# A Perceiver block with 16 experts: layer-norm rows ahead of their low parts, the last expert rows sent by the load queue, shared down products in four banks

## The chip, the cores and the metric

The kernel runs on one core of one Trainium2 chip, in one launch. The metric is the time of the whole program on the device in microseconds (us), the median of several runs. On the core five engines run at once, each with its own instruction stream, and wait for each other only on semaphores: TensorE (PE, matrix products; its weight loads are listed apart as PEld), VectorE (DVE), ScalarE (ACT), GpSimd (POOL) and SyncE (SP, which here does nothing but issue DMAs). A DMA is issued by the sequencer of an engine into that engine's own queue ("SPq", "ACTq") and carried out by 16 DMA engines that all queues share. PSUM, where PE writes its products, has 8 banks of 512 floats for each of 128 partitions.

## The reference

Three residual steps on `x` (8 batches of 64 tokens, width 512): a cross attention over 512 context rows, a linear attention, and a mixture of experts. The change lies in the third and in the layer norm before it.

```python
x = x + xattn(layernorm(x), ctx, ctx)
x = x + linear_attention(layernorm(x))       # ends in  out @ w_out + b_out
x = x + ffn(layernorm(x))

def ffn(h):                                  # E = 16 experts, cap = 8 tokens of each batch for each expert
    scores = softmax(h @ gate_w.T).transpose(0, 2, 1)
    topk_w, topk_idx = top_k(scores, cap)
    x_tok = take_along_axis(h, topk_idx)     # 64 slots (8 batches x 8) for each expert
    g, u = x_tok @ Wg[e].T, x_tok @ Wu[e].T  # 512 -> 1024
    eo = (gelu(g) * u) @ Wd[e].T * topk_w    # 1024 -> 512
    out = scatter_add(eo at topk_idx)
    shared = (gelu(h @ Ws_g.T) * (h @ Ws_u.T)) @ Ws_d.T
    return out + shared
```

## The kernel before, in words

All engines' programs are written out by hand, in order. The 512 tokens stand as NT = 4 tiles of 128.

**From the second attention to the router.** PE multiplies `att_T` by `w_out` tile by tile (`residual`, L1217) into banks 4 to 7. For each tile DVE (`residual_ln`) adds the bank to `x` (L723), takes the statistics (`ln_stats`, L703 to L705), has ACT take a square root (`ln_std`, L457), and finishes the normalised rows `xn_moe` (`ln_rows`, L711 to L715). PE transposes a tile's rows into bank t (`moe_transpose`, L1321). Products that need more precision than one pass gives are made of two parts: ACT copies the transposed tile rounded into `xn_hi` (`xn_high_tile`, L462), and DVE subtracts that from the bank into `xn_lo_moe` (`xn_low_tile`, L735). In DVE's program the low part of tile t-1 stands between the statistics and the rows of tile t (argument `behind`). Then PE makes 48 small products of the router (L1399, 32 columns each; those of tile t wait for its low part), DVE picks the tokens, and PE gathers them into `x_slot`.

**The items.** What follows is a list of 24 items: one eighth of the shared network ("shared item", s0 to s7) and the 16 experts (e0 to e15), in the order s0, e0, e1, s1, e2, e3, s2, ..., e12, e13, s7, e14, e15. Item n writes its gate product into bank 2*(n%2) and its up product into the bank after it; ACT takes the gelu (L638), DVE multiplies (L949). For an expert PE transposes the result (L1365, bank 4 + n%2), ACT copies it into `hid_T` (L654) and PE multiplies by `w_d` (L1376, bank 6 + n%2). For a shared item PE makes 4 down products of 3 passes each, one for each token tile (L1389), and DVE adds each to `x` (`item_sum`, L965, semaphore `sx_done`). They go into banks 4 + n%2 and 6 + n%2 in turn, so the third waits for the sum of the first and the fourth for the sum of the second. PE's order in a step is gate of n, transposes of n-1, up product of n, down product of n-1.

**The loads.** SP issues three loads of 2 MB for each expert (`expert_load`, L394), each as soon as PE has used the buffer of the expert two before. The very last is `w_d` of e15, after the down product of e13.

**The rows.** An expert's output (64 slots by 512) must be regrouped by batch: 8 small DMAs, one for each batch b, of 8 rows of 2 KB each into `eo_slot[:, b]`. The place of `eo_slot[:, b]` holds the low parts of the shared weights of s_b until that item is done, so a batch's rows can be sent only from then on. ACT issues them (`send`, L649) between its other work. In its program, after the cast of s7's hidden part and before the copy into `hid_T` of e14, stand 21 of them: b = 7 of e0 to e12, and all 8 of e13. The 8 of e14 come after it, then gelu of e15. When all have landed PE multiplies by `give` (L1469), which puts the rows of 15 experts back to their tokens; then come the transposes, the down product and the `give_last` product (L1476) of e15, DVE's last sums and the output.

```python
            def shared_down_bank(n, t):
                return (4, 6)[t % 2] + n % 2
```

Of the kernel before, what the change touches and what calls it, by code (L numbers as in the profile page):

```python
# [25 lines left out]
NT = TOK // P  # L26
# [12 lines left out]
def perceiver_block(nc, x_d, ctx_d, wq_d, bq_d, wk_d, bk_d, wv_d, bv_d, wo_d, bo_d, wqkv_d, proj_d,  # L39
                    wout_d, bout_d, gate_d, wg_d, wu_d, wd_d, wsg_d, wsu_d, wsd_d, out_d):  # L40
    main = ExitStack()
    with main:
# [292 lines left out]
        def experts_upto(n):  # L335
            return n + 1 - shared_before(n + 1)
# [3 lines left out]
            return experts_upto(n) + NT * shared_before(n + 1)  # L340

        def shared_down_bank(n, t):
            return (4, 6)[t % 2] + n % 2

        def qkv_bank(n):
            return n % 4 if n < 8 else n - 4
# [7 lines left out]
        @block.sync  # L354
        def _(sp):
            for dt in range(KT):
                sp.dma_start(wk_raw[:, dt], wk_d[:, dt]).then_inc(wk_in[dt], 16)
                sp.dma_start(ctx_raw[:, dt], ctx_d[0, :, dt]).then_inc(ctx0_in[dt], 16)
            for tile, src in ((bias_k, bk_d), (bias_q, bq_d), (bias_v, bv_d)):
                sp.dma_start(tile[:], src).then_inc(bias_in, 16)  # L360
            sp.dma_start(wv_raw[:], wv_d).then_inc(wv_in, 16)
            sp.dma_start(x[:], x_d.rearrange("(t p) d -> p t d", p=P)).then_inc(x_in, 16)
            sp.dma_start(wq_raw[:], wq_d).then_inc(wq_in, 16)
            sp.dma_start(bo_rows[:], bo_d.partition_broadcast(P)).then_inc(rows_in, 16)
            with sp.Fori(1, B) as b:
                sp.wait_ge(ctx_split, b + KT - 1)
                sp.dma_start(ctx_raw[:], ctx_d[b]).then_inc(ctx_in, 16)
            sp.dma_start(w_o[:], wo_d).then_inc(wo_in, 16)
            sp.dma_start(w_qkv[:], wqkv_d).then_inc(wqkv_in, 16)
            sp.wait_ge(x_done, NT)  # L370
            sp.dma_start(bout_rows[:], bout_d.partition_broadcast(P)).then_inc(rows_in, 16)
            for q in range(4):
                sp.dma_start(proj_twice[HD * q:HD * (q + 1)], proj_d[q % 2]).then_inc(proj_in, 16)
            sp.dma_start(w_out[:], wout_d).then_inc(wout_in, 16)
            sp.wait_ge(xbias_done, 2 * NT)
            sp.dma_start(gate[:], gate_d).then_inc(gate_in, 16)
            sp.wait_ge(qkv_lo_dve, KT)
            sp.wait_ge(qkv_lo_pool, 2 * KT)
            sp.dma_start(ws_g[:], wsg_d).then_inc(wsg_in, 16)
            sp.wait_ge(kv_ps, NT * KT)  # L380
            sp.dma_start(ws_u[:], wsu_d).then_inc(wsu_in, 16)
            sp.dma_start(w_u0[:], wu_d[0]).then_inc(wu_in[0], 16)
            sp.dma_start(w_d0[:], wd_d[0]).then_inc(wd_in[0], 16)
            sp.dma_start(ws_d[:], wsd_d).then_inc(wsd_in, 16)
            sp.wait_ge(att_done, 2 * NT)
            sp.dma_start(w_g0[:], wg_d[0]).then_inc(wg_in[0], 16)
            def expert_load(kind, e):

                tiles, src, arrived, used = {"g": (w_g, wg_d, wg_in, g_ps), "u": (w_u, wu_d, wu_in, u_ps),
                                             "d": (w_d, wd_d, wd_in, down_ps)}[kind]  # L390
                if e >= 2:
                    n = AT["e", e - 2]
                    sp.wait_ge(used, downs_upto(n) if kind == "d" else n + 1)
                sp.dma_start(tiles[e % 2][:], src[e]).then_inc(arrived[e % 2], 16)  # L394

            expert_load("g", 1)
            expert_load("u", 1)
            for e in range(2, E, 2):
                for kind, ahead in (("g", 0), ("u", 0), ("g", 1)):
                    expert_load(kind, e + ahead)  # L400
                if e == 2:
                    sp.wait_ge(give_ps, 2)
                    sp.wait_ge(last_T_done, NT)
                    expert_load("d", 1)
                for kind, ahead in (("d", 0), ("u", 1), ("d", 1)):
                    expert_load(kind, e + ahead)
            for t in range(NT):
                sp.wait_ge(y_done, t + 1)
                sp.dma_start(out_d[P * t:P * (t + 1), :], x[:, t, :]).then_inc(out_sent, 16)
            sp.wait_ge(out_sent, 16 * NT)  # L410
# [42 lines left out]
        def _(act):  # L453
# [171 lines left out]
            act.wait_ge(wsd_in, 16)  # L625
            shared_high_gu(0)
            shared_high_d(0)
            for t in range(NT):
                ln_std(2, (t,))
                if t:  # L630
                    xn_high_tile(t - 1)
            xn_high_tile(NT - 1)
            act.wait_ge(lsub_done, 1)
            act.activation(logit[:], logit[:], ACT.Exp).then_inc(lexp_done, 1)

# [3 lines left out]

            def send(n):  # L640

                ready, free = experts_upto(n - 1), shared_before(n + 1)
                was_ready, was_free = experts_upto(n - 2), shared_before(n)
                for e in range(ready):
                    if e >= was_ready:
                        act.wait_ge(eo_done, e + 1)
                    for b in range(0 if e >= was_ready else was_free, free):
                        row = SLOTS * (e % 2) + CAP * b
                        act.dma_start(eo_slot[CAP * e:CAP * (e + 1), b, :], eo_of(e)[row:row + CAP, :]).then_inc(eo_sent[e % 2], 16)  # L649

            def item_out(n):
                if is_expert(n):
# [31 lines left out]
                if split_next:  # L684
                    shared_high_d(earlier[1] + 1)
            item_out(LAST - 1)
            send(LAST)
            item_gelu(LAST)
            item_out(LAST)

# [2 lines left out]
        def _(dve):  # L693
# [21 lines left out]
                dve.tensor_scalar(xn[:, t, :], x[:, t, :], mean_var[:, t, 0:1], r,  # L715
                                  ALU.subtract, ALU.mult).then_inc(xn_done, 1)

            def residual_ln(k, xn, behind=None):

                for t in range(NT):  # L720
                    dve.wait_ge(xbias_done, NT * (k - 1) + t + 1)
                    dve.wait_ge(res_ps, NT * (k - 1) + t + 1)
                    dve.tensor_tensor(x[:, t, :], bank(RES_BANK[k - 1] + t), x[:, t, :], ALU.add).then_inc(x_done, 1)  # L723
                    dve.wait_ge(x_done, NT * (k - 1) + t + 1)
                    ln_stats(t)
                    if behind and t:
                        behind(t - 1)
                    ln_rows(k, t, xn)
                if behind:
                    behind(NT - 1)  # L730

            def xn_low_tile(t):
                toks = slice(P * t, P * (t + 1))
# [202 lines left out]
            dve.tensor_tensor(gate_lo[:], gate[:], gate_hi[:].bitcast(F32), ALU.subtract).then_inc(gate_split, 1)  # L936
            shared_low_gu(0)
            shared_low_d(0)
            residual_ln(2, xn_moe, xn_low_tile)


            def over_experts(v):
# [114 lines left out]
        def _(pe):  # L1057
# [156 lines left out]
            def residual(k, rows_T, w, behind=None):  # L1214
                for t in range(NT):
# [1 line left out]
                        ins = pe.matmul(bank(RES_BANK[k] + t), rows_T[:, dt, P * t:P * (t + 1)], w[:, dt, :],  # L1217
                                        start=(dt == 0), stop=(dt == KT - 1))
                    ins.then_inc(res_ps, 1)
                    if behind and t:  # L1220
                        behind(t - 1)

            pe.wait_ge(o_done, B)
            pe.wait_ge(wo_in, 16)
# [96 lines left out]
                    ins = pe.transpose(ps[:, t, P * dt:P * (dt + 1)], xn_moe[:, t, P * dt:P * (dt + 1)], ident[:])  # L1321
                ins.then_inc(xnT_ps, 1)

            residual(1, att_T, w_out)
            for t in range(NT):
                moe_transpose(t)

            def item_up(n, weights, shared_parts, off, in_, done, steps=range(KT)):


                dst = 2 * (n % 2) + off
                if is_expert(n):
                    e = ITEMS[n][1]
                    pe.wait_ge(in_[e % 2], 16 * (e // 2 + 1))
# [33 lines left out]
            def item_down(n):  # L1368
# [11 lines left out]
                else:  # L1380
                    i = ITEMS[n][1]
                    pe.wait_ge(ws_split, 3 * i + 3)
                    pe.wait_ge(hid_split, shared_before(n) + 1)
                    for t in range(NT):
                        if t >= 2:
                            pe.wait_ge(sx_done, NT * shared_before(n) + t - 1)
                        rows = slice(P * t, P * (t + 1))
                        for j, (a, c) in enumerate(((hid_hi, ws_d_hi[:]), (hid_lo, ws_d_hi[:]), (hid_hi, ws_d_lo[:, i, :]))):
                            ins = pe.matmul(bank(shared_down_bank(n, t)), a[:, n % 2, rows], c, start=(j == 0), stop=(j == 2))  # L1389
# [136 lines left out]
```

## Time and profile before

| | |
|---|---|
| median of 3 runs | 713.93 us (712.55 to 715.34) |
| the profiled execution's own time | 714.17 us |
| its span, first to last instruction | 712.4 us |
| PE busy | 661.5 us, 93% of the span |
| DVE busy, ACT busy | 318.2 us, 250.8 us |
| mean granted TensorE clock | 0.971 |

The span is what the trace covers; the 1.8 us more are start and end outside of it. Busy shares are means over stages with different limits, so the stages around the change are read one by one. "Granted clock" is 1.00 at TensorE's full 2.4 GHz and 0.50 at 1.2 GHz.

### The profile page before, as it was taken

Reading aid. Unit: us, or ns where it says so; the run is one execution under the profiler, and the core shown is the slowest. Engines: PE = TensorE matmul, PEld = TensorE weight load, DVE = VectorE, ACT = ScalarE, POOL = GpSimd, SP = SyncE. Lnnn points to the kernel's source line nnn. Section 1 sums busy time; section 2 is a strip of 40 time slices with the busy share of each in tenths; the row PEclk is TensorE's granted clock in tenths of the full one; section 3 lists DMA queues with packets and bytes.
Section 4 is the critical chain, followed back from the end, with each engine's and each line's share of the span. In section 5 each row is a group of like instructions: output and inputs, shape, how many; then the busy total and the mean of one; then the engine's idle time right before and its main releaser. Section 6 shows DMA issues by size and latency. Waiting matters only on the chain.

```text
span 712.4 us, 10361 instructions
## 1 busy us (share of the span) xinstructions
PE 661.5 (93%) x4224; PEld 427.2 (60%) x4224; DVE 318.2 (45%) x646; ACT 250.8 (35%) x479; POOL 31.8 (4%) x33
## 2 busy tenths in 40 slices
PE   6999999999999999799989499989999999999966
PEld 5767778777787875578875285353544434354422
DVE  5965554636445165657786532423233231323302
ACT  4644545536454351547752113111220221122000
POOL 0300000000000000750000000000000000000000
PEclk9999999999999999899999769999999999999989
DMA  8111101010700000311196200889999999999921
GB/s 300 69 60 60 49 13 60 1 61 1 296 0 2 1 2 1 104 47 76 28 428 276 97 0 15 339 352 422 424 405 403 409 404 396 398 386 390 367 73 61
DMA packets 14347, 129.55 MB, mean 182 GB/s; under 512 B 2720, under 2 KB 2848, under 8 KB 6240
## 3 DMA queue, kind: packets, MB, share of 16 engines
q1 hardware_dynamic: 12384, 126.95, 45.3%
q10 hardware_dynamic: 1920, 1.97, 0.9%
q8 instruction: 33, 0.54, 0.3%
q14 instruction: 10, 0.08, 0.0%
HBM read 125.90 MB, written 1.05 MB: 178 GB/s over the span
## 4 chain that ended last, share of the span: by engine, by line
PE 78%; DVE 10%; ACT 4%; DMA 2%; ACTq 2%; issue 2%; SPq 1%; DVEq 0%
PE ps L1072 21%; PE ps L1337 14%; PE ps L1376 8%; PE ps L1347 5%; PE ps L1253 4%; PE ps L1142 4%; PE ps L1389 3%; PE ps L1217 2%; PE ps L1118 2%; ACTq L649 2%; PE ps L1153 2%; PE ps L1183 2%; PE ps L1290 2%; PE ps L1399 1%; PE ps L1302 1%
## 5 line engine op out<-in xcount | busy, mean ns | idle before, releaser
L1376 PE MATMUL ps<-w_d,hid_T 128*64 128x512 f32 x256 | 59.6, 609 | 9.6 <-ACT hid_T L654 8.2
L1337 PE MATMUL ps<-w_g,x_slot 128*64 128x512 f32 x256 | 58.1, 595 | 0.7 <-ACT x_slot L673 0.7
L1337 PE MATMUL ps<-w_u,x_slot 128*64 128x512 f32 x256 | 58.0, 595 | 0.0
L503 ACT ACTIVATE probs<-ps,neg_max 128x512 f32<-128x512 f32 x64 | 43.5, 686 | 39.1 <-DVE neg_max L788 39.1
L638 ACT ACTIVATE hid<-ps 128x512 f32<-128x512 f32 x24 | 14.3, 598 | 113.9 <-PE ps L1337 79.6
L768 DVE COPY probs_T<-ps 128x512 f32<-128x512 f32 x32 | 22.1, 692 | 68.7 <-PE ps L1142 68.7
L1072 PE MATMUL ps<-wv_hi,ctx_hi 128*128 128x512 f32 x128 | 51.6, 403 | 0.2 <-ACT v_s L484 0.2
L1072 PE MATMUL ps<-wv_lo,ctx_hi 128*128 128x512 f32 x128 | 50.0, 391 | 0.0
L1072 PE MATMUL ps<-wv_hi,ctx_lo 128*128 128x512 f32 x128 | 49.9, 390 | 0.0
L788 DVE TENSOR_REDUCE neg_max<-ps 128x1 f32<-128x512 f32 x64 | 39.7, 683 | 18.4 <-PE ps L1118 18.3
L949 DVE TENSOR_TENSOR hid<-hid,ps 128x512 f32<-128x512 f32 x24 | 16.5, 686 | 70.2 <-PE ps L1337 34.3
L1376 PEld LDWEIGHTS ps<-w_d,hid_T 128*64 128x64 f32 x256 | 18.1, 140 | 45.2 <-issue 35.9
L1072 PE MATMUL ps<-ctx_hi,wk_hi 128*128 128x512 f32 x112 | 44.4, 397 | 0.4 <-ACT k_T L488 0.4
L1072 PE MATMUL ps<-ctx_lo,wk_hi 128*128 128x512 f32 x112 | 43.6, 390 | 0.0
L1072 PE MATMUL ps<-ctx_hi,wk_lo 128*128 128x512 f32 x112 | 43.6, 389 | 0.0
L1337 PEld LDWEIGHTS ps<-w_g,x_slot 128*64 128x64 f32 x256 | 17.9, 137 | 35.4 <-issue 34.3
L488 ACT ACTIVATE k_T<-ps,bias_k 128x512 f32<-128x512 f32 x32 | 21.6, 689 | 48.8 <-PE ps L1072 48.8
L1337 PEld LDWEIGHTS ps<-w_u,x_slot 128*64 128x64 f32 x256 | 18.0, 137 | 33.5 <-issue 33.5
L667 ACT COPY x_slot<-ps 64x512 f32<-64x512 f32 x14 | 8.1, 580 | 80.8 <-PE ps L1376 80.8
L1072 PEld LDWEIGHTS ps<-wv_hi,ctx_hi 128*128 128x128 f32 x128 | 24.0, 188 | 16.6 <-ACT v_s L484 6.3
L781 DVE TENSOR_SCALAR probs<-probs,row_inv 128x512 f32<-128x512 f32 x64 | 31.1, 487 | 2.3
L1142 PE MATMUL ps<-ident,probs 128*128 128x128 f32 x256 | 31.0, 274 | 0.0
(218 smaller groups left out, 1215.2 us busy)
## 6 DMA issues: line engine op xcount, KB each, us to landing
w_u<-in_wu SPq DMA_DIRECT2D x16, 2048.0 KB, 15.3
w_d<-in_wd SPq DMA_DIRECT2D x16, 2048.0 KB, 11.3
w_g<-in_wg SPq DMA_DIRECT2D x16, 2048.0 KB, 12.5
ctx_raw<-in_ctx SPq DMA_DIRECT2D x7, 1024.0 KB, 4.8
w_qkv<-in_wqkv SPq DMA_DIRECT2D x1, 3072.0 KB, 15.2
ws_g<-in_wsg SPq DMA_DIRECT2D x1, 2048.0 KB, 7.8
ws_u<-in_wsu SPq DMA_DIRECT2D x1, 2048.0 KB, 7.8
ws_d<-in_wsd SPq DMA_DIRECT2D x1, 2048.0 KB, 21.9
```

Source lines behind the costliest of these rows:

```text
L488: act.activation(k_T[:, ht, :], bank(FIRST_K + ht if first else PROJ[ht % 2]), ACT.Identity, bias=bias_k[:, ht:ht + 1], scale=1.0).then_in ...
L503: act.activation(probs[:, p, :], bank(SCORE[p]), ACT.Exp, bias=neg_max[:, p:p + 1], scale=1.0, accum_out=row_sum[:, p:p + 1]).then_inc(exp ...
L768: dve.tensor_copy(probs_T[:, ht % 2, 1].rearrange("p s c -> p (s c)"), bank(TRANS[ht % 2][1])).then_inc(pT_done[1], 1)
L781: dve.tensor_scalar(probs[:, p, :], probs[:, p, :], row_inv[:, p:p + 1], None, ALU.mult).then_inc(prob_done, 1)
L788: dve.tensor_reduce(neg_max[:, p:p + 1], bank(SCORE[p]), AX.X, ALU.max, negate=True).then_inc(max_done, 1)
L1072: ins = pe.matmul(dst, a(dt), c(dt), start=(dt == 0 and i == 0), stop=(dt == KT - 1 and i == 2))
L1142: ins = pe.transpose(ps[:, TRANS[ht % 2][pr], P * st:P * (st + 1)], probs[:, 2 * ht + pr, P * st:P * (st + 1)], ident[:])
L1253: ins = pe.matmul(bank(qkv_bank(n)), a, c, start=(dt == 0 and i == 0), stop=(dt == KT - 1 and i == 2))
L1337: ins = pe.matmul(ps[64 * fh:64 * (fh + 1), dst, :], x_slot[:, e, dt, :], weights[e % 2][:, dt, BANK * fh:BANK * (fh + 1)], start=(dt == 0 ...
L1347: ins = pe.matmul(bank(dst), a, c[:, dt, :], start=(dt == 0 and j == 0), stop=(dt == KT - 1 and j == 2))
L1376: ins = pe.matmul(ps[64 * fh:64 * (fh + 1), 6 + n % 2, :], hid_T[:, n % 2, j, 64 * fh:64 * (fh + 1)], w_d[e % 2][:, KT * fh + j, :], start ...
L1389: ins = pe.matmul(bank(shared_down_bank(n, t)), a[:, n % 2, rows], c, start=(j == 0), stop=(j == 2))
```

## The change

Three places, independent of each other. (1) DVE makes the rows of all four tiles before any low part, ACT's square roots and high copies are interleaved to match, and PE transposes tile 0 between the third and the fourth tile of the `w_out` product. (2) The 21 rows named above and the 8 of e14 are issued by SP, behind the last load. (3) The four down products of a shared item go to four banks: the item's own gate and up banks, and 4 + n%2, 6 + n%2. The waits between them are gone; in their place the gate product of item n+2, which writes to the first of these banks, waits until the first two sums of item n are done.

```diff
         def shared_down_bank(n, t):
-            return (4, 6)[t % 2] + n % 2
+            return (2 * (n % 2), 2 * (n % 2) + 1, 4 + n % 2, 6 + n % 2)[t]
+
+        LATE = E - 3
+
+        def send_row(queue, e, b):
+            row = SLOTS * (e % 2) + CAP * b
+            queue.dma_start(eo_slot[CAP * e:CAP * (e + 1), b, :], eo_of(e)[row:row + CAP, :]).then_inc(eo_sent[e % 2], 16)
...
                 for kind, ahead in (("d", 0), ("u", 1), ("d", 1)):
                     expert_load(kind, e + ahead)
+            sp.wait_ge(g_ps, AT["s", NF - 1] + 1)
+            for e in range(E - 1):
+                sp.wait_ge(eo_done, e + 1)
+                for b in range(0 if e >= LATE else B - 1, B):
+                    send_row(sp, e, b)
             for t in range(NT):
                 sp.wait_ge(y_done, t + 1)
...
-            for t in range(NT):
-                ln_std(2, (t,))
-                if t:
-                    xn_high_tile(t - 1)
-            xn_high_tile(NT - 1)
+            ln_std(2, (0, 1))
+            xn_high_tile(0)
+            ln_std(2, (2,))
+            xn_high_tile(1)
+            ln_std(2, (3,))
+            xn_high_tile(2)
+            xn_high_tile(3)
...
             def send(n):
 
-                ready, free = experts_upto(n - 1), shared_before(n + 1)
+                ready, free = min(experts_upto(n - 1), LATE), min(shared_before(n + 1), B - 1)
                 was_ready, was_free = experts_upto(n - 2), shared_before(n)
...
             item_out(LAST - 1)
-            send(LAST)
             item_gelu(LAST)
             item_out(LAST)
...
                     ln_stats(t)
-                    if behind and t:
-                        behind(t - 1)
                     ln_rows(k, t, xn)
-                if behind:
-                    behind(NT - 1)
...
-            residual_ln(2, xn_moe, xn_low_tile)
+            residual_ln(2, xn_moe)
+            for t in range(NT):
+                xn_low_tile(t)
...
                     ins.then_inc(res_ps, 1)
-                    if behind and t:
-                        behind(t - 1)
+                    if behind and t == 2:
+                        behind(0)
...
-            residual(1, att_T, w_out)
-            for t in range(NT):
+            residual(1, att_T, w_out, moe_transpose)
+            for t in range(1, NT):
                 moe_transpose(t)
 
             def item_up(n, weights, shared_parts, off, in_, done, steps=range(KT)):
 
 
                 dst = 2 * (n % 2) + off
+                if n >= 2 and not is_expert(n - 2):
+                    pe.wait_ge(sx_done, NT * shared_before(n - 2) + 2)
...
                     pe.wait_ge(hid_split, shared_before(n) + 1)
+                    if shared_before(n):
+                        pe.wait_ge(sx_done, NT * shared_before(n))
                     for t in range(NT):
-                        if t >= 2:
-                            pe.wait_ge(sx_done, NT * shared_before(n) + t - 1)
```

DVE's program at the second tile of the layer norm before the experts, before (`std` is ACT's square root, `xn_hi_done` counts ACT's high copies):

```order
L723 TENSOR_TENSOR x<-ps,x 128x512 [waits res_ps,xbias_done]
L703 BN_STATS stats<-x 128x6 [waits x_done]
L704 BN_AGGR mean_var<-stats 128x2 [waits dve_chain]
L705 TENSOR_SCALAR var_eps<-mean_var 128x1 [waits dve_chain]
L735 TENSOR_TENSOR xn_lo_moe<-ps,xn_hi 128x4x128 [waits xn_hi_done]
L711 RECIPROCAL rstd<-std 128x1 [waits std_done]
```

The same place in the changed kernel, and the end of the stage:

```order
L734 TENSOR_TENSOR x<-ps,x 128x512 [waits res_ps,xbias_done]
L714 BN_STATS stats<-x 128x6 [waits x_done]
L715 BN_AGGR mean_var<-stats 128x2 [waits dve_chain]
L716 TENSOR_SCALAR var_eps<-mean_var 128x1 [waits dve_chain]
L722 RECIPROCAL rstd<-std 128x1 [waits std_done]
...
L726 TENSOR_SCALAR xn_moe<-x,mean_var,rstd 128x512 [waits dve_chain]
L742 TENSOR_TENSOR xn_lo_moe<-ps,xn_hi 128x4x128 [waits xn_hi_done] x4
```

The low part no longer stands ahead of the rows; all four stand behind the last rows. On PE the transposes of tile 0 have moved ahead of the last four `w_out` products (the trace lists each of these products as two):

```order
L1226 MATMUL ps<-w_out,att_T 128x512 x11
L1330 MATMUL ps<-ident,xn_moe 128x128 [waits xn_done]
L1330 MATMUL ps<-ident,xn_moe 128x128 x3
L1226 MATMUL ps<-w_out,att_T 128x512 x4
L1330 MATMUL ps<-ident,xn_moe 128x128 [waits xn_done]
```

ACT's program after the up product of s7, before:

```order
L657 CAST hid_hi<-hid 128x512 [waits hid_done]
L649 DMA eo_slot<-x_slot 8x512 x13
L649 DMA eo_slot<-x_slot 8x512 [waits eo_done]
L649 DMA eo_slot<-x_slot 8x512 x7
L654 COPY hid_T<-ps 128x512 [waits hidT_ps]
L667 COPY eo<-ps 64x512 [waits down_ps]
L649 DMA eo_slot<-eo 8x512 [waits eo_done]
L649 DMA eo_slot<-eo 8x512 x7
L638 ACTIVATE hid<-ps 128x512 [waits g_ps]
```

SP's program from the last load on, now:

```order
L400 DMA w_d<-in_wd 128x4096 [waits down_ps]
L349 DMA eo_slot<-x_slot 8x512 [waits eo_done,g_ps]
L349 DMA eo_slot<-x_slot 8x512 [waits eo_done] x13
L349 DMA eo_slot<-x_slot 8x512 x7
L349 DMA eo_slot<-eo 8x512 [waits eo_done]
L349 DMA eo_slot<-eo 8x512 x7
L420 DMA out<-x 128x512 [waits y_done] x4
```

All 29 DMAs have left ACT's program, where the copy into `hid_T` now follows the cast directly, and stand in SP's between the last load and the output.

## Rows read from the trace of the kernel before

**Rows 1.** The page, part 1: busy time, share and instructions of each engine.
```profile
...
PE 661.5 (93%) x4224; PEld 427.2 (60%) x4224; DVE 318.2 (45%) x646; ACT 250.8 (35%) x479; POOL 31.8 (4%) x33
...
```

**Rows 2.** Windows: length, busy us of PE, PEld, DVE, ACT, POOL; PEclk, DMA share, GB/s.
```profile
...
286.50:290.10 3.60, 0.67 (x5) 0.42 (x4) 2.56 (x10) 2.93 (x7) 1.26 (x1) 0.98 0.70 189
290.10:296.90 6.80, 6.11 (x15) 4.82 (x16) 2.94 (x6) 3.94 (x9) 6.61 (x5) 0.51 0.54 171
...
408.00:418.30 10.30, 10.30 (x50) 10.30 (x50) 0.69 (x1) 1.87 (x2) 0.00 (x0) 0.50 0.00 0
418.30:423.20 4.90, 4.90 (x15) 3.62 (x16) 2.12 (x9) 1.54 (x2) 0.00 (x0) 0.51 0.00 0
480.00:660.00 180.00, 179.04 (x809) 81.08 (x805) 50.93 (x76) 35.23 (x65) 0.00 (x0) 1.00 1.00 403
...
```

**Rows 3.** Timeline of DVE, second layer norm: start, duration, instruction, idle before.
```profile
...
385.08 0.69 DVE L723 TENSOR_TENSOR x<-ps,x 128x512 f32<-128x512 f32 x1 [1.56 <-PE ps L1217]
...
396.37 0.69 DVE L735 TENSOR_TENSOR xn_lo_moe<-ps,xn_hi 128x512 fp32r<-128x512 f32 x1 [6.03 <-ACT xn_hi L462]
...
```

**Rows 4.** Timeline of PE, same stretch.
```profile
...
395.11 0.60 PE L1321 MATMUL ps<-ident,xn_moe 128*128 128x128 f32 x4
...
407.31 1.12 PE L1321 MATMUL ps<-ident,xn_moe 128*128 128x128 f32 x4 [3.34 <-DVE xn_moe L715]
408.08 0.38 PE L1399 MATMUL ps<-gate_hi,xn_hi 128*128 128x32 f32 x1
...
```

**Rows 5.** Timeline, first layer norm of this form, from 275 us.
```profile
...
275.01 0.69 DVE L723 TENSOR_TENSOR x<-ps,x 128x512 f32<-128x512 f32 x1 [3.87 <-PE ps L1217]
...
285.31 0.69 DVE L723 TENSOR_TENSOR x<-ps,x 128x512 f32<-128x512 f32 x1
...
288.84 0.66 PE L1062 MATMUL ps<-ident,xn_lin 128*128 128x128 f32 x4 [2.33 <-DVE xn_lin L715]
...
```

**Rows 6.** Timeline of SP after that: four small DMAs in a row.
```profile
...
286.40 1.82 SPq L373 DMA_DIRECT2D proj_twice<-in_proj  x4
...
```

**Rows 7.** The chain that ended last, one shared item: start, us, work.
```profile
...
533.20 2.79 PE ps L1347 x12
...
546.44 0.91 PE ps L1389 x3
548.18 1.65 PE ps L1389 x6
549.83 3.58 PE ps L1337 x16
...
```

**Rows 8.** Timeline of the tail, from 668 us.
```profile
...
668.80 13.41 ACTq L649 DMA_DIRECT2D eo_slot<-x_slot  x20
...
674.77 0.60 PE L1365 MATMUL ps<-ident,hid 128*128 128x128 f32 x4
...
682.90 5.14 PE L1376 MATMUL ps<-w_d,hid_T 128*64 128x512 f32 x16 [7.53 <-ACT hid_T L654]
...
688.70 0.68 DVE L972 TENSOR_TENSOR eo<-ps,eo 64x512 f32<-64x512 f32 x1 [13.04 <-ACT eo L667]
...
689.41 5.26 ACTq L649 DMA_DIRECT2D eo_slot<-eo  x8
...
696.07 3.65 PE L1469 MATMUL ps<-eo_slot,give 120*64 120x512 f32 x16 [1.17 <-DMA eo_slot<-eo]
...
```

**Rows 9.** DMA issues, windows 654.8:655.3 and 664.6:664.8; last column: issue to landing.
```profile
...
w_d<-in_wd SPq DMA_DIRECT2D x1, 2048.0 KB, 18.1
w_u<-in_wu SPq DMA_DIRECT2D x1, 2048.0 KB, 23.3
...
w_d<-in_wd SPq DMA_DIRECT2D x1, 2048.0 KB, 19.5
...
```

**Rows 10.** DMA view of the whole run: a queue, and an issue with its landing.
```profile
...
q10 hardware_dynamic: 1920, 1.97, 0.9%
...
out<-x SPq DMA_DIRECT2D x4, 256.0 KB, 2.0
...
```

More of the change, by code:

```diff
@@ L647, in send @@
                     for b in range(0 if e >= was_ready else was_free, free):
-                        row = SLOTS * (e % 2) + CAP * b
-                        act.dma_start(eo_slot[CAP * e:CAP * (e + 1), b, :], eo_of(e)[row:row + CAP, :]).then_inc(eo_sent[e % 2], 16)
+                        send_row(act, e, b)
             def item_out(n):
@@ L716, in ln_rows, with residual_ln @@
                                   ALU.subtract, ALU.mult).then_inc(xn_done, 1)
-            def residual_ln(k, xn, behind=None):
+            def residual_ln(k, xn):
                 for t in range(NT):
```

## The prediction, made before the run

> **What bounds the kernel now.** The page first [rows 1]: PE is busy 93% of the span. So a gain must come from the holes in PE's row or from stretches at half clock. I looked for both with the windows view and then read the timelines there.
>
> The windows [rows 2] show that from 480 to 660 us PE is busy 179.0 of 180 us while the DMA engines are at share 1.00 and move 403 GB/s. Two resources are full at once there, so I must ask of every PE saving in that stretch whether the loads can follow. They also show that the router's products (408.0 to 418.3) and the first shared products (to 423.2) run at granted clock 0.50.
>
> The second layer norm: DVE sits idle 6.03 us before the first low part, released by ACT's high copy [rows 3]. That copy waits for the transposes of tile 0, which PE reaches only after all `w_out` products, at 395.11 [rows 4]. Everything behind, the rows of tiles 1 to 3 included, is queued on DVE behind a low part that no one needs yet. The last transposes start at 407.31, the router at 408.08 [rows 4].
>
> The tail [rows 8]: after the cast of s7 ACT issues 20 DMAs in 13.41 us (one more stood before the cast); PE has finished the transposes of e14 at 675.4 and waits 7.53 us for `hid_T`. The 16 products after that take 5.14 us where 16 of this size take 3.65 in the row at 696.07: the clock had fallen. Then 1.17 us of waiting for e14's rows. After 696.07 all is a fixed chain to the end.
>
> **Part 1, layer norm.** The kernel has the same stage without low parts once already, at 275 us [rows 5]: adds at 275.01 and 285.31, so 3.43 us a tile, and the last transposes start at 288.84, which is 13.83 us after the first add. Here the first add is at 385.08 [rows 3], and nothing ahead of it changes: 398.9. The transposes of tile 0, moved between the third and fourth tile's `w_out` products, push the fourth by their 0.60 us [rows 4]: 399.5. High copies of tiles 1 and 2 on ACT fall between its square roots, ahead of need (the roots need 0.2 us, the copies 0.6). The low part of tile 0 (0.69 us) starts when the last rows end, about 399.4, and is done at 400.1; the router follows its transposes by 0.77 us (408.08 - 407.31): 400.3. Gain 408.08 - 400.3 = **7.8 us**. The other low parts, 0.7 us apart, stay ahead of the router's 12 products a tile (2.6 us at half clock).
>
> Does it come with clock? The idle gaps get shorter: from about 396.9, when the transposes of tiles 1 and 2 are done, to 399.5, where the last of several gaps before was 3.34 us [rows 4]. But the first layer norm has just this shape (0.67 us of PE work in 3.6 us) and the clock fell right after it, to 0.51 over the next 6.8 us [rows 2], and 10.3 us of uninterrupted router products did not raise it. I count no clock gain, with 1.7 us either way for where the fall and the rise happen to lie. The Trainium skill ("TensorE: Matmul & The Clock Gate", section "HAM oscillation — how this bites in real kernels") says that an idle PE is throttled back and that keeping gaps short avoids it; read plainly that speaks for full clock here, and it is a rival below.
>
> **Part 2, the rows.** ACT's copy can follow the transposes at once. From the end of its DMAs (668.80 + 13.41 = 682.21) to the product at 682.90 it took 0.7 us [rows 8]; from the end of the transposes that gives 675.4 + 0.7 = 676.1: 6.8 us, and 1.5 us more because the clock has no idle stretch to fall in (5.14 - 3.65). Together **8.3 us**. SP has nothing else to do there but wait for the end. Its issue of a small DMA costs 1.82 / 4 = 0.46 us [rows 6] against 0.66 on ACT (5.26 / 8, [rows 8]).
>
> **Part 3, the banks.** In the chain a shared down product runs from 546.44 to 549.83, 3.39 us for 12 passes, with the hole after the first six; 12 passes of this size without one take 2.79 us [rows 7], up to 2.9 with the start after other operands. So 0.5 us each, 8 times: **4.1 us**. The new wait is hidden: the third product could start 1.74 us after the first (548.18 - 546.44), when the first sum was done; a sum takes 0.7 us (the same add) [rows 3], so the second is done at 2.4 us, and the gate product that waits for it comes at 2.9. Without that cover it would cost what DVE is late by.
>
> **What is late next: the loads.** For the tail I use the clock of the trace of before with the 7.8 us of part 1 taken off, since loads shift with the uses that release them. The load queue never runs dry after 480, so its landings do not follow PE's later savings, only the first (0.5 us). `w_d` of e14 lands 18.1 us after 654.9, at 673.0, that of e15 19.5 us after 664.7, at 684.2 [rows 9]. Neither shares the engines with the 21 rows any more, of which some 6 ran before the first of the two landed. What does a row DMA cost the stream? Below: the ACT queue's packets took 0.9% of the engines' span for 120 rows, 0.009 x 712.4 / 120 = 0.05 us [rows 10]. Above: 0.66 us, the pace at which e14's 8 rows were issued without piling up [rows 8]. Between: the two loads from 673.0 to 684.2 took 11.2 us where 403 GB/s gives 10.4, with some 14 rows beside them: 0.06. I take 0.06. Then `w_d` of e14 lands about 672.1, just when PE wants it (676.1 - 4.1 = 672.0), and the last load at 684.2 - 0.5 - 21 x 0.06 = 682.4.
>
> PE: down of e14 672.1 to 675.6 (16 products, 3.5 us between starts of such groups), gate and up of e15 to 682.5 (before, from 688.0 to 696.07 less 1.17 us of waiting: 6.9 us). DVE has e14's output 1.4 us after the down product (before 688.70 + 0.68 against 688.0), at 677.0; SP sends 8 in 3.7 to 5.3 us; a row lands 1.4 us after its issue (before: 689.41 + 5.26 = 694.7 to 696.07), so 683.7 at the latest if the queue were empty. It isn't: all 29 rows stand behind the last load in its own queue, where loads land in the order of issue. 682.4 + 29 x 0.06 = 684.2. So PE waits about 1.7 us there instead of 1.17. **Loss 0.5 us.** The skill's "DMA: Bandwidth & Descriptors", section "Queues, rings and completion order", has the rule: each DMA engine takes its queues in turn but consumes one queue in ring order. It speaks against this part of the change, since rows of the ACT queue could pass the loads and these cannot; the loads' order in this trace agrees.
>
> **Sum.** 7.8 + 8.3 + 4.1 - 0.5 = 19.7 us. The check from the other end: `give` at 684.2 instead of 696.07 is 11.9, plus 7.8 is 19.7 too. The profiled execution took 714.17, so 694.5; it lies 0.24 above the median 713.93, so **694.2 us**.
>
> **Rivals.**
> - *The loads become the bound* and part 3 comes to nothing. `w_u` of e15 now takes 23.3 us to land and `w_d` of e14 18.1 [rows 9], growing through the stage; a stream a few per cent slower makes PE wait what it saved. For it: DMA share 1.00. Against: PE never waited from 480 to 660. 694.2 + 4.1 = 698.3. Chance 12%.
> - *Full clock through the router* (the skill's rule above). The router's 10.3 us halve and the 4.9 us after it lose 2.4: 694.2 - 5.1 - 2.4 = 686.7. Against: the first layer norm. 6%.
> - *SP cannot run ahead*: its rows are not taken while loads are queued, so 29 x 0.46 = 13.3 us of issue start at 682.4; rows land at 697.1, PE waits 12.9 more. 707.1. Against: ACT's 20 went out at an even 13.41 / 20 = 0.67 us while loads were queued [rows 8]. 6%.
> - *Slower than before*: rows do not overlap in the load queue and each takes what an output tile takes from issue to landing, 2.0 us [rows 10]. 682.4 + 58 = 740.4, 56 us later than 684.2: 750.4. It decides from (684.2 + 19.7 - 682.4) / 29 = 0.74 us a row. Against: the ACT queue took rows every 0.66 us. 2%.
> - *The change doesn't do what it says*: the holes are set by something else (DVE's own pace, late `hid_T`), each part gives under a fifth. About 710. 3%.
> - The forecast: 71%.
>
> **How the numbers follow.** The likeliest case spans part 1 from 6 to 9.5 (the clock's phase), part 3 from 2 to 4.8, and the rows' cost from 0.05 to 0.27 us (up to 29 x 0.21 = 6 us later for the last, less what the load wins): 690 to 699. That takes in the rival of the loads. I give 689.5 to 699.5. A measurement of this kernel tells 0.5%, 3.6 us, from no change. Faster by more than that: 0.95 (all but the last two rivals); within: 0.03; slower: 0.02.
>
> **What would show it.** Right: in the DVE timeline no idle above 0.5 us between first add and last rows; router start near 400.3; ACT's `hid_T` of e14 within a microsecond of its transposes, and no PE idle above 2 us from there to the end; shared down products of 2.9 us. Wrong: PE waiting for `w_d` or `w_u` before 664, a gap before `give` of more than 4 us, row DMAs on SP with long pauses between them, or a gate product waiting for DVE's sums.

## The result, and the profile after

The changed kernel takes **701.16 us** in the median (700.81 to 701.96, 4 runs) against 714.02 us for the kernel before on the same chip: ratio 0.982, 95% interval 0.980 to 0.984. It is 12.9 us faster; the forecast was 19.7 us, 694.2 us with a range up to 699.5. The direction was right, the size was 7.0 us too good.

Part 1 of the page of the changed kernel, against [rows 1]:

```profile
span 699.7 us, 10378 instructions
PE 660.3 (94%) x4224; PEld 428.4 (61%) x4224; DVE 318.4 (46%) x646; ACT 251.1 (36%) x479; POOL 31.8 (5%) x33
```

PE's work is the same to 1.2 us; what went are holes. The second layer norm, timeline of DVE and PE (beside [rows 3, 4]):

```profile
384.97 0.69 DVE L734 TENSOR_TENSOR x<-ps,x 128x512 f32<-128x512 f32 x1 [1.56 <-PE ps L1226]
391.56 0.60 PE L1330 MATMUL ps<-ident,xn_moe 128*128 128x128 f32 x4
395.71 0.69 DVE L734 TENSOR_TENSOR x<-ps,x 128x512 f32<-128x512 f32 x1 [0.39 <-PE ps L1226]
398.64 0.55 DVE L726 TENSOR_SCALAR xn_moe<-x,mean_var,rstd 128x512 f32<-128x512 f32 x1
399.10 2.60 DVE L742 TENSOR_TENSOR xn_lo_moe<-ps,xn_hi 128x512 fp32r<-128x512 f32 x4
399.24 1.12 PE L1330 MATMUL ps<-ident,xn_moe 128*128 128x128 f32 x4 [2.76 <-DVE xn_moe L726]
400.01 0.38 PE L1410 MATMUL ps<-gate_hi,xn_hi 128*128 128x32 f32 x1
```

The 6.03 us hole of DVE is gone, its largest idle time between the first add and the last rows is 0.39 us, and the router starts at 400.01 instead of 408.08. Its products still run at half clock. Windows of the changed kernel (length, busy us of PE, PEld, DVE, ACT, POOL, granted clock, DMA share, GB/s):

```profile
400.00:410.00 10.00, 10.00 (x49) 10.00 (x48) 1.67 (x3) 1.87 (x2) 0.00 (x0) 0.50 0.00 0
415.00:420.00 5.00, 5.00 (x18) 3.53 (x17) 4.07 (x26) 0.60 (x1) 0.00 (x0) 0.87 0.00 0
```

A shared down product in the chain that ended last, in one piece now (in [rows 7] 3.39 us with a hole):

```profile
506.40 2.96 PE ps L1400 x12
```

The tail, beside [rows 8] (SPq is the issuing of DMAs on SP):

```profile
653.96 0.33 SPq L400 DMA_DIRECT2D w_d<-in_wd  x1
654.39 14.17 SPq L349 DMA_DIRECT2D eo_slot<-x_slot  x21
664.86 3.65 PE L1387 MATMUL ps<-w_d,hid_T 128*64 128x512 f32 x16 [0.67 <-ACT hid_T L666]
669.89 6.57 SPq L349 DMA_DIRECT2D eo_slot<-eo  x8
680.88 6.14 PE L1480 MATMUL ps<-eo_slot,give 120*64 120x512 f32 x16 [5.50 <-DMA eo_slot<-eo]
688.28 3.65 PE L1387 MATMUL ps<-w_d,hid_T 128*64 128x512 f32 x16 [0.68 <-ACT hid_T L666]
692.82 3.67 PE L1487 MATMUL ps<-hid,give_last 128*128 128x512 f32 x8 [0.89 <-DVE hid L977]
```

The wait for `hid_T` fell from 7.53 to 0.67 us. In its place the `give` products (L1480) wait 5.50 us for the rows of e14, where they waited 1.17, and then take 6.14 us, where these 16 took 3.65: the clock falls during the wait (the granted clock is 1.00 until 679.1 and 0.50 from there to 685.9). The last row is issued at 675.84 and lands at 680.84. In the text below a *row* is one of these 16 KB DMAs, the *last load* is `w_d` of e15, and a landing is the last semaphore increment that the DMA engines make for it, read from the trace's semaphore events.

### The profile page after: what moved, and what is told of

It is laid out like the page before. It is cut to its first block, busy times and chain, and to the rows that moved or that the text cites. A ratio compares the mean times of both kernels' runs of the same rounds, so it can differ in the third digit from the quotient of the medians.

```text
span 699.7 us, 10378 instructions
## 1 busy us (share of the span) xinstructions
PE 660.3 (94%) x4224; PEld 428.4 (61%) x4224; DVE 318.4 (46%) x646; ACT 251.1 (36%) x479; POOL 31.8 (5%) x33
## 4 chain that ended last, share of the span: by engine, by line
PE 82%; DVE 8%; ACT 4%; DMA 3%; SPq 2%; issue 1%; DVEq 0%; ACTq 0%
PE ps L1081 22%; PE ps L1348 15%; PE ps L1387 8%; PE ps L1358 6%; PE ps L1262 4%; PE ps L1151 4%; PE ps L1400 3%; PE ps L1226 3%; PE ps L1127 2%; PE ps L1162 2%; PE ps L1192 2%; PE ps L1299 2%; PE ps L1410 1%; PE ps L1311 1%; PE ps L1436 1%; DMA w_d<-in_wd 1%
## 5 line engine op out<-in xcount | busy, mean ns | idle before, releaser
L1387 PE MATMUL ps<-w_d,hid_T 128*64 128x512 f32 x256 | 58.2, 596 | 2.8 <-DMA w_d<-in_wd 1.5
```

The lines of the kernel that those rows point to most:

```text
L1387: ins = pe.matmul(ps[64 * fh:64 * (fh + 1), 6 + n % 2, :], hid_T[:, n % 2, j, 64 * fh:64 * (fh + 1)], w_d[e % 2][:, KT * fh + j, :], start ...
```

## The experiments

Two theories on the 5.50 us. **Q**: each row costs the DMA engines that carry it far more than 0.06 us; they stand behind the last load and end one after the other. **Issue**: the pace or place of the issue on SP (0.67 us a row) sets the landing; the expectations call it rival I. Each kernel was timed beside the kernel before, whose median lay between 714.0 and 714.6 us.

**One part alone** (three runs; each is the kernel before with that part of the diff).

Only the layer norm:

> The kernel before with the layer-norm part alone. My theory, that the three parts are independent and this one shifts all that follows: router start at about 400.0 instead of 408.1, and the whole 8.1 us reach the end, about 706. Rival, that the tail gives part of it back because loads are released by something that did not move: 708 to 711.

Measured 706.36 us (704.42 to 707.67), ratio 0.988 (0.986 to 0.990): 8.0 us gained. The tail is that of before, 7.84 us of waiting for `hid_T` included.

Only the rows on SP:

> The kernel before with the row DMAs moved to SP alone. Theory Q (rows stand behind the last load in one queue and each takes 0.2 us of it): the product of e14 starts near 676.1 instead of 682.9, the last load lands near 683.3, the last row 29 x 0.2 = 5.8 us after it, near 689, PE waits 2 to 3 us; about 7 us gained, 707. Rival I (SP's slow issue of e14's rows, 0.8 us each, sets the end): the last row lands a fixed 4.4 us after its issue, so near 692, about 4 us gained, 710.

Measured 708.76 us, ratio 0.992 (0.990 to 0.994): 5.6 us, 2.2 us less than 8.3 - 0.5. The time lies between the two expectations; the last row lands at 688.29, near Q's 689 and not the rival's 692. `give` waits 2.8 us and then takes 5.35.

Only the banks:

> The kernel before with the four banks alone. If PE is the bound of the item stage: each shared down product 2.9 instead of 3.4 us, 8 times, and since ACT's 21 row DMAs start from the cast of s7 they move along: about 4 us gained, 710. If the loads are the bound: PE waits for w_d or w_u late in the stage, under 2 us gained, 712 or more.

Measured 710.90 us, ratio 0.995 (0.993 to 0.997): 3.4 us, which is the 8 x 0.43 us of 3.39 - 2.96. The three add to 17.0 us, the whole change gives 12.9. So something is lost between the parts.

**The change without the banks.**

> The changed kernel without the four banks (layer norm and rows only). My theory now: the DMA engines set the end of the changed kernel (last load plus 29 rows), and they do not follow what PE saves in the items. Then the banks are worth nothing beside the other two: 700.5 to 702, as the full change. Rival, that the parts simply add and the loss lies elsewhere: 3.4 us more than the full change, 704.5.

Measured 700.20 us (698.04 to 702.54), ratio 0.980 (0.977 to 0.982): the same as the whole change. Its `give`:

```profile
681.15 5.35 PE L1478 MATMUL ps<-eo_slot,give 120*64 120x512 f32 x16 [2.74 <-DMA eo_slot<-eo]
```

It starts at the same time and waits 2.74 us instead of 5.50. The last load lands at 675.37, against 675.07 with the banks. So the banks' 3.4 us are spent in front of a transfer that does not come sooner. Part 3 is worth nothing beside the other two.

**The eight rows of e14 from ACT's queue.**

```diff
-            for e in range(E - 1):
+            for e in range(E - 2):
                 sp.wait_ge(eo_done, e + 1)
...
             item_out(LAST - 1)
+            act.wait_ge(eo_done, E - 1)
+            for b in range(B):
+                send_row(act, E - 2, b)
             item_gelu(LAST)
```

> The changed kernel with the 8 rows of e14 issued by ACT again, the other 21 by SP behind the last load. Theory Q: the 21 still drain at 0.2 us each behind the load that lands near 675.1, so the wait before give ends near 675.1 + 21 x 0.2 = 679.3 or a little later (the 8 share the same DMA engines), against 680.9: under 2 us gained, 699.5 to 701. Rival I (SP's issue pace of e14's rows sets the end): ACT issues them in 5.3 us from 669.9, they land near 676.6, PE hardly waits and its clock does not fall: 4.3 + 2.4, near 694.5.

Measured 699.96 us (698.15 to 701.82), ratio 0.980 (0.977 to 0.983):

```profile
668.66 5.26 ACTq L349 DMA_DIRECT2D eo_slot<-eo  x8
679.37 6.21 PE L1483 MATMUL ps<-eo_slot,give 120*64 120x512 f32 x16 [5.21 <-DMA eo_slot<-eo]
```

The issue ends at 673.9, and the wait is nearly as long. The last load lands at 673.58, the last row at 679.32, 5.74 us = 29 x 0.198 later. `give` starts 1.5 us earlier than in the changed kernel because the load lands 1.5 us earlier; the wait behind the load is the same. The issue is not the cause. The prediction cited the Trainium skill, "DMA: Bandwidth & Descriptors", section "Queues, rings and completion order": an engine takes its queues in turn. Read as "rows of another queue pass the load" it does not help here: `give` waits for all 29 rows, 21 of them stay behind the load, and the last landing comes after the same 29 x 0.2 us.

**Thirteen rows left out.** The rows of batch 7 of experts 0 to 12 are not sent, and the product of batch 7 reads batch 6's rows instead.

```diff
-                for b in range(0 if e >= LATE else B - 1, B):
+                for b in range(0, B if e >= LATE else 0):
                     send_row(sp, e, b)
```

> The changed kernel without the 13 rows of batch 7 of e0 to e12; the product of batch 7 reads batch 6's rows in their place, so those 13 DMAs are left out of the work and nothing else. Theory Q: the last row lands 16 x 0.2 = 3.2 us after the last load instead of 5.8: give near 678.3, 2.6 us gained, 698.5. Rival I (the end is set by the issue of e14's rows or a fixed time after it): the issue of e14's 8 rows does not move, give stays near 680.9, 701.

Measured 696.81 us (696.33 to 698.70), ratio 0.977 (0.973 to 0.980). The last load lands at 672.95, the last of 16 rows at 676.19: 16 x 0.20. The issue theory, with `give` near 680.9, falls; Q's price is confirmed:

```profile
676.23 5.35 PE L1480 MATMUL ps<-eo_slot,give 120*64 120x512 f32 x16 [2.32 <-DMA eo_slot<-eo]
```

The gain against the changed kernel's 701.16 is 4.3 us, more than the 2.6 expected. Not all of it belongs to the rows: in the profiled execution the last load was already issued 1.5 us earlier (652.49 against 653.96), and `give` runs 0.8 us shorter.

**Other orders on SP.** First 21 rows ahead of the last load and e14's on ACT:

```diff
-                    expert_load(kind, e + ahead)
+                    if (kind, e + ahead) != ("d", E - 1):
+                        expert_load(kind, e + ahead)
...
-            for e in range(E - 1):
+            for e in range(E - 2):
...
+            expert_load("d", E - 1)
...
+            act.wait_ge(eo_done, E - 1)
+            for b in range(B):
+                send_row(act, E - 2, b)
```

> The changed kernel with SP's 21 rows issued ahead of the last load (w_d of e15) and e14's 8 rows issued by ACT. Theory Q (0.2 us a row on the busiest DMA engines, whatever the queue; only what stands ahead counts): w_u of e15 lands near 668, the 21 rows by 672.3, e14's rows go between the packets of the last load and land near 676 to 677; the last load lands near 680, when PE needs it at 682. PE waits 2 to 3 us instead of 5.5 and its clock may hold: 696 to 698. Rival (the order in the queue does not matter, rows land when all the engines' work is done): 680, as before, 700 to 701.

Measured 700.75 us, ratio 0.981 (0.979 to 0.984). The load, issued at 662.3, lands at 679.1, and the rows of e14, issued on ACT from 670.5 to 675.8, at 680.3. Q's expectation missed here: it had these rows at 676 to 677 and the time at 696 to 698, and the time is the rival's. The DMA records show their packets between 674.6 and 679.0, among those of the load, which end at 678.5: they are taken in turn with the load's, but the last one still comes with the load's end. So Q holds as a price for rows that stand behind the load, not as a rule that another queue avoids it. Then 21 rows, the load, and e14's 8 rows, all on SP:

> As the one above, but e14's rows stay on SP behind the last load. Theory Q: they wait for the load in their own queue, and the sum of work ahead of them is the same 29 rows and the same loads: give near 680.9, no gain, 700 to 702. Rival (a row costs only when it is behind a load, so moving 21 of them ahead shortens the end): 4 us gained, 697.

Measured 700.56 us, ratio 0.981 (0.979 to 0.984); the load lands at 679.5, `give` starts at 681.15, as Q expected. As long as e14's rows come after the load, the order of the rest moved nothing in these three kernels.

**The last load behind all 29 rows.** `give` needs all rows, and the last load is needed only after `give`, so this is the order of use.

> The changed kernel with one transfer moved: the last load (w_d of expert 15) is issued by SP behind all 29 rows instead of ahead of them; nothing is left out. Theory Q (what is in the DMA engines ahead of the rows sets when they land, and they cost 0.20 us each there): the rows no longer stand behind the load's 2 MB, so those of expert 14 (issued from 669.9) land within 2 to 3 us of the last issue, near 677 to 678, the give matmuls begin there instead of at 680.9 and, with a shorter idle time ahead of them, nearer to 3.65 than to 6.14 us. The load is issued near 676 and has the engines for itself: at the 400 GB/s of the page 2 MB are 5.3 us, with 2 us of latency it lands near 683.5; the down product of expert 15 begins at about 684 instead of 688.3, and the median is near 697. Rival A (a load takes its 18 to 25 us from issue to landing whatever is beside it): it lands after 694 and the time is 706 or more. Rival B (the rows' landing is bound by the rate of their issue): give not before 680, no gain.

Measured **695.93 us** (694.52 to 697.86), ratio 0.974 (0.972 to 0.976):

```profile
670.84 5.29 SPq L349 DMA_DIRECT2D eo_slot<-eo  x8
676.18 0.44 SPq L400 DMA_DIRECT2D w_d<-in_wd  x1
677.53 3.65 PE L1482 MATMUL ps<-eo_slot,give 120*64 120x512 f32 x16 [1.18 <-DMA eo_slot<-eo]
684.34 3.65 PE L1389 MATMUL ps<-w_d,hid_T 128*64 128x512 f32 x16 [2.57 <-DMA w_d<-in_wd]
```

`give` runs at full clock after 1.18 us of waiting, and the load takes 8.0 us from issue to landing, not 21: the other 13 are gone with the transfers that stood ahead of it. The median is 1 us under the expected 697. With four of e14's rows on ACT and four on SP, so that the load is issued earlier:

```diff
-                    expert_load(kind, e + ahead)
+                    if (kind, e + ahead) != ("d", E - 1):
+                        expert_load(kind, e + ahead)
...
-                for b in range(0 if e >= LATE else B - 1, B):
+                for b in range({E - 2: B // 2, LATE: 0}.get(e, B - 1), B):
                     send_row(sp, e, b)
+            expert_load("d", E - 1)
...
+            act.wait_ge(eo_done, E - 1)
+            for b in range(B // 2):
+                send_row(act, E - 2, b)
```

> As load_last, and the eight rows of expert 14 are issued by two queues, four by ACT and four by SP. Theory Q: the issues of the rows end near 673 instead of 676, the load is issued 2.5 us earlier and lands near 681.5; rows land near 676; the down product of expert 15 is then ready after give, its transposes and the copy, near 683, and the median is 695 to 697, 0 to 2 us below load_last. Rival A: 703 or more. Rival B as for load_last.

Measured **693.97 us** (688.94 to 695.13), ratio 0.969 (0.967 to 0.972), the best kernel here: 20.6 us under the 714.6 of before in these runs, and 1 us better than the lower end of what was expected.

```profile
673.51 0.65 SPq L400 DMA_DIRECT2D w_d<-in_wd  x1
676.73 3.65 PE L1485 MATMUL ps<-eo_slot,give 120*64 120x512 f32 x16 [0.39 <-DMA eo_slot<-eo]
681.93 3.65 PE L1392 MATMUL ps<-w_d,hid_T 128*64 128x512 f32 x16 [0.96 <-DMA w_d<-in_wd]
```

**Rows on POOL's queue.** The 13 rows of batch 7 (the edit moves their loop from SP to POOL, with a semaphore of its own):

> The changed kernel with the 13 rows of batch 7 issued by POOL's queue instead of SP's, the 16 rows of experts 13 and 14 and the last load as they were; nothing is left out. On the HWDGE queues a transfer of 8 partitions lies on 8 of the 16 DMA engines. Theory Q with this imbalance: if POOL's queue spreads its transfers over other engines than SP's, the busiest ones have 13 x 0.20 = 2.6 us less behind the load at best and 1.3 us less if they alternate, rows land 1.3 to 2.6 us earlier, and the time is 698 to 700. Rival (the issue or the work of POOL's transfers costs more than SP's): the rows land no earlier, 701 or more.

Measured 697.94 us (696.35 to 700.22), ratio 0.976 (0.975 to 0.978). The load lands at 676.02, the last of the 16 rows that SP sends at 679.26: again 0.20 us each, and POOL's 13 rows were down at 670.34, ahead of the load. The kernel is 3.2 us faster than the changed one, with 16 rows behind the load instead of 29, although PE waits 1.96 us for `w_d` of e14, which it did not in the changed kernel. Together with the order of `load_last_2q`:

> load_last_2q with the 13 rows of batch 7 on POOL's queue; nothing is left out. If in load_last_2q the last load's own landing (8.3 us after its issue at 673.5) sets the end, the rows' engines do not matter any more: 693.5 to 694.5, the same as load_last_2q. If the engines of the rows still hold the last load up, it lands 1 to 2.6 us earlier and the time is 692.

Measured 695.17 us (694.39 to 696.39), ratio 0.974 (0.972 to 0.975), no better than the order alone (0.967 to 0.972), and outside both expectations.

All 104 rows of experts 0 to 12 on POOL. This was to explain a thing in the trace of the changed kernel: the last load's 16 increments, one from each DMA engine, come in two groups. (Its theory I is on these groups, and not the issue theory of above.)

```
665.41 665.55 666.64 666.88 667.23 667.32 667.37 667.68   672.38 672.41 673.03 673.52 673.70 673.85 674.42 675.07
```

> The changed kernel with all 104 rows of experts 0 to 12 on POOL's queue instead of ACT's and SP's; the last load and the 16 rows of experts 13 and 14 as they were. Theory I (eight of the 16 DMA engines carry all rows and are 7 us behind at the last load, of whose 16 engine increments eight come by 667.7 and eight from 672.4 to 675.1): with rows spread over 16 engines the increments come together, near (667 + 674) / 2 = 671, the rows behind end 16 x 0.20 = 3.2 us later at 674.5, give need not wait after the up product at 675.4, and with 5.5 us of waiting and 2.5 us of slow clock gone the time is 693 to 694. Rival W (the eight engines are slower for a reason other than the rows, or POOL's transfers cost the stream more): the increments stay 5 us or more apart and the time is 697 or more, as pool_b7.

Measured 699.00 us (695.48 to 701.38), ratio 0.978 (0.975 to 0.980). The increments are still in two groups, 667.1 to 668.6 and 673.4 to 676.6, and the time is rival W's. So taking the rows off the queues of ACT and SP does not end the lag. That the rows do not cause it is not shown: no trace tells which engines carried POOL's rows. In `load_last_2q`, where the last load is alone, all 16 come within 0.9 us (680.91 to 681.79), so these engines are not slow by themselves. The lag is not made at the end either. In the changed kernel first and last increment of a load lie 0.9 us apart for the load that lands at 443, 1.8 at 470, 2.7 at 500, 4.7 at 579 and 9.7 at 675; in the kernel with 104 rows on POOL it grows alike, to 9.5. It grows while the rows are sent, but why stays open. The last of the 16 SP rows again ends 3.15 us after the load. With the tail's better order:

> pool_all with the order of the tail of load_last_2q (rows of experts 13 and 14 ahead of the last load, four of expert 14 on ACT). Theory I: rows land by 676.3 without a wait of PE, the last load is bound by its own issue at 673.5 and lands near 681.5: 693 to 694, no better than pool_all or load_last_2q. Rival: below 692, then something in the stream before was still held up by the rows.

Measured 698.69 us, ratio 0.979 (0.977 to 0.981), 5 us above the 693 to 694 expected and slower than the same order with the rows on ACT and SP. `give` waits 3.8 us in both of these kernels. In the second the rows of e14 are issued by 671.6 and land only at 677.3; what holds them is not shown.

**Tile 0's transposes back behind the product.**

```diff
-            residual(1, att_T, w_out, moe_transpose)
-            for t in range(1, NT):
+            residual(1, att_T, w_out)
+            for t in range(NT):
```

> The changed kernel with the four transposes of tile 0 back behind the second attention projection, as the kernel before has them; nothing is left out. The prediction's term of 0.6 us was that the early transposes push the last two projection tiles, and so the residual adds of DVE, by 0.6 us; against that 2 tiles' worth of transposes stand between the third low part and the router. If the chain of DVE sets the router's start, as the trace of the changed kernel shows (2.76 us idle ahead of the last four transposes), the router starts 0.4 to 0.6 us earlier and the time is 0.3 to 0.9 us less, 700.5. Rival: the transposes of tile 0 then fall behind the idle time and the slower clock is reached differently, the router starts no earlier, 701 to 702.

Measured 704.11 us (701.19 to 705.63), ratio 0.984 (0.982 to 0.986): not faster. By the medians it is 3 us slower, though the interval of its ratio touches that of the changed kernel (0.980 to 0.984). The expectation was wrong, and DVE and ACT show why:

```profile
394.18 0.15 DVE L716 TENSOR_SCALAR var_eps<-mean_var 128x1 f32<-128x1 f32 x1
396.31 0.59 ACT L473 CAST xn_hi<-ps 128x512 fp32r<-128x512 f32 x1 [5.17 <-PE ps L1330]
396.79 0.21 ACT L468 ACTIVATE std<-var_eps 128x1 f32<-128x1 f32 x1
397.03 0.16 DVE L722 RECIPROCAL rstd<-std 128x1 f32<-128x1 f32 x1 [2.69 <-ACT std L468]
```

The square root of tile 2 could run at 394.3, but stands in ACT's queue behind the high copy of tile 0, which waits for the transposes. DVE is idle 2.69 us, and the router starts at 402.61, 2.6 us later than in the changed kernel. The early transposes cost 0.6 us and save this. Whether the square root ahead of the copy would do it without them was not run.

## Why the prediction was right in direction and wrong in size

- **Layer norm, 7.8 us: right.** The router starts 8.07 us earlier (forecast 400.3, measured 400.01), the part alone gives 8.0. The clock was called right too: 0.50 in the router although the gaps were shorter, as the first layer norm had shown, and against the advice of the Trainium skill ("TensorE: Matmul & The Clock Gate", section "HAM oscillation — how this bites in real kernels") to keep gaps short, read plainly: the last gap was 2.76 us instead of 3.34, and the clock was at half all the same.
- **Rows off ACT, 8.3 us: right as far as it goes.** `hid_T` follows its transposes at once, e14's down product runs in 3.65 us and starts at 664.86; with the 8.07 us of part 1 added back that is 672.9, forecast 672.1.
- **Banks, 4.1 us: size slightly off, and no gain in the whole.** 0.43 us each instead of 0.5, 3.4 us alone, nothing beside the other two. The rival that sent part 3 to nothing had its outcome right, by another way: not a stream of loads that grew slower, but the rows behind the last load.
- **SP can run ahead of its queue: right.** 21 rows go out in 14.17 us with the load in flight. The price of an issue was not right: 0.67 us, not 0.46.
- **The step that failed: "Loss 0.5 us", and in it the 0.06 us a row.** On the forecast's clock (8.07 us added back) the last load lands at 683.1 instead of 682.4, and `give` starts at 688.95 instead of 684.2. Of these 4.7 us, 0.7 are the load and 29 x (0.20 - 0.06) = 4.0 the rows. Both ways to 0.06 averaged over 16 engines: [rows 10] is a share of 16 engines' time, and the 11.2 us between two landings held rows only beside a full stream. But the wait ends with the last engine to finish. A row has 8 partitions and 16 packets, 8 of 2 KB and 8 of 4 bytes. The Trainium skill, "DMA: Bandwidth & Descriptors", section "Why a DMA increments its semaphore by 16 and not by 1", says that a transfer whose slowest dimension is 8 uses 8 of the 16 engines, on the queues of SP and ACT always the lowest-numbered. The eight packets of each kind agree with eight engines; which ones no run shows. Eight engines instead of 16 double the 0.05. The other factor of two is in the DMA records: a row's 2 KB packet takes 0.088 us on average where rows go between the loads (560 to 640 us), but 0.154 from 674 to 678 us, where the rows behind the load run out, and 0.19 to 0.20 for the last three. So a price read inside the stream does not hold behind it; what slows the packets there stays open. The range's upper row price, 0.27, did hold the 0.20, but its own 6 us added to 694.2 are 700.3, and the range still ended at 699.5.
- **What was left out: the clock in the new wait.** The sum counted 1.5 us back because a gap went, and did not ask what the new gap would do. It costs 6.14 - 3.65 = 2.5 us. 4.7 + 2.5 = 7.2 us, less the 0.27 us that part 1 gave above its 7.8, for 7.0 us measured. The list of what would make the forecast wrong did name it: a gap before `give` of more than 4 us.

## What to carry to other kernels

When many small transfers share the DMA engines with big loads, price one by the time between the last landings of a series of them behind the loads (here 0.20 us), not by its share of all engines, and count all that stand behind the last load. Issue the last transfers in the order in which they are used: moving one load behind the rows that are needed before it gave 5.2 us, moving e14's rows to ACT's queue 1.2, within the noise, and moving 13 rows to POOL's queue, which took them out from behind the load, 3.2. Where several savings all end at one transfer, only the first of them counts, so test each part beside the others and not only alone; and a wait that is new can take the clock with it.

## What the runs showed of the hardware

The price of a row at the end of the stream, from landings of the last load and of the last row behind it:

| kernel | rows behind | load lands | last row lands | us a row |
|---|---|---|---|---|
| changed | 29 | 675.07 | 680.84 | 0.199 |
| rows_only | 29 | 682.54 | 688.29 | 0.198 |
| ln_rows | 29 | 675.37 | 681.11 | 0.198 |
| e14_on_act | 29 | 673.58 | 679.32 | 0.198 |
| no_b7 | 16 | 672.95 | 676.19 | 0.203 |
| pool_b7 | 16 | 676.02 | 679.26 | 0.203 |
| pool_all | 16 | 676.62 | 679.77 | 0.197 |

The duration of the 16 `give` products by PE's idle time ahead of them: after 0.39 us and 1.18 us 3.65 us; after 2.32 us 5.35; after 2.66 us 5.06; after 2.74 and 2.76 us 5.35; after 3.75 us 5.35; after 3.85 us 6.26; after 4.33 us 6.50; after 5.21 us 6.21; after 5.50 us 6.14; after 5.79 us 5.54. So every wait above 2.3 us cost 1.4 to 2.9 us here and none below 1.2 did, but a longer wait did not cost more. At half clock throughout they would take 7.3, twice 3.65, by my estimate.

A 2 MB load with no other load beside it takes 8.0 to 8.4 us from issue to landing (the last load of load_last, load_last_2q, combo and pool_all_2q). The last three of a full stream take 18 to 27: 18.1, 23.3 and 19.5 in the kernel before, 20.5, 25.0 and 21.1 in the changed one, 22.0, 26.9 and 23.4 in pool_all.
